# Sorting with the features stationary, a mixer tap on ScalarE, and direct turns at the end of a layer

## The chip, the cores and the metric

The program runs on one core of a Trainium2 chip, in one launch. A core has five engines that run their own instruction queues side by side and meet through semaphores: TensorE (PE, matrix products), VectorE (DVE), ScalarE (ACT), GpSimd (POOL) and SyncE (SP, which here only starts transfers). The metric is the device time of one execution in microseconds (us), compared as the median of several.

## The reference, cut to what matters

```python
x = x + quantised_product(layernorm(x), ctx)              # 1: int8-like fake quantisation, matmul
x = x + mixer(layernorm(x), ...)                          # 2: state-space mixer, 8 groups of 16 heads
x = x + experts(layernorm(x), ...)                        # 3: base matmul + top-2 of 8 LoRA experts
x = x + cloud(ctx, layernorm(x), ...)                     # 4: point cloud network, two layers
x = x + block_sparse_linear(layernorm(x), ...)            # 5
x = x + gated_ffn(layernorm(x), ...)                      # 6

# inside the mixer: a causal convolution with 4 taps, then silu
xBC = silu(conv(xBC, conv_w, groups=CONV_DIM) + conv_b)
L = exp(segment_sum(A * dt))                              # per head, 64 x 64, per batch
# inside the cloud: 4 sort orders of 1024 points from Morton and Hilbert keys of the coordinates
inds = [window(argsort(key)) for key in keys]             # windows of 10 neighbours in sorted order
g = [concat(center, feats[inds] - center) for inds ...]   # 1024 points x 10 rows x 512 channels
out = softmax(q @ q.T / 8) @ q ; fused = out @ W_lin.T + b
h = lrelu(instance_norm(conv1x1(fused))).max(over the 10)
```

The mixer sees T = 128 tokens (2 batches of 64) and the cloud 2 batches of 1024 points with 64 features each.

## The kernel before, in words

Every stage is a block of its own, one instruction stream for each engine, written by hand; nothing is scheduled by a tool. A block ends when all engines have reached its end (a barrier). Waits on semaphores (`pe.wait_ge(s_x, n)`) set the order between the engines. `hold_clock` (L100) issues idle products of the identity on PE, in fives (HOLD = 5), to keep PE's granted clock up.

**Stage 1** computes the quantised product; at its end PE runs 8 x HOLD idle passes of two each while DVE adds the result to x and takes the norm's statistics.

**Mixer.** PE projects the normalised x by the streamed weights (L530) for two B and two C chunks of 4 blocks and then for each of the 8 groups for two halves of x (bank 0 and 1) and two halves of the gate. ACT copies each projected chunk out of PSUM into a padded buffer (L643 `xpad`) and signals `s_evac`; DVE convolves the 4 taps of 4 blocks, 16 instructions a chunk: the newest tap with the bias by L751, the three others by L753. A chunk of PSUM may be written again once `s_evac` has come. `segments()` (L572) makes the cumulative sums of the decays as two products of 128x512, whose right side `seg_rhs` GpSimd builds from `adt_tok`. `out_projection` (L560) multiplies by `w_out`, streamed into `wt`. DVE also computes the 30-bit sort keys in between (class `SortKeys`, small chained instructions on 128x32 integers), three bits in the head, two inside group 0 and four bits and the final assembly between group 0 and group 1; `parg`, the parameters of a group, is copied at a group's start (L810). Ranks are counted by DVE within groups 1 to 7 (L781). Groups 1 to 6 are a loop.

**Experts.** 32 base products (L973), then the transposed `mid` and the adapters (L979).

**Cloud, layers 1 and 2.** The layer opens with the products of the layer's weights (L1388 to L1391), then sorts. A sort is a product with one-hot matrices: DVE builds 64 one-hots of 128 x 1024 (L1633: `iota == rank`), and PE multiplies for each of 8 phases (batch, method) 8 chunks of points by 8 chunks of ranks in two parts (high and low half of the float), with the one-hot as the stationary side and 64 feature columns moving (L1416: 128 products of 64 columns a phase). ACT evicts each phase (L1547). After four phases PE transposes the result (L1427) into `sortedT`, in which features lie on partitions and ranks run along the row. 32 transfers put the unsorted rows into `fTr`.

Then 43 steps of 24 points run as a software pipeline. For step it: POOL subtracts the centre (L1765 `X`), PE computes scores (L1453) and turned rows (L1466), DVE takes the maximum and subtracts it (L1679, L1681), ACT takes exp (L1582), DVE the sums (L1701) and reciprocals, POOL normalises (L1783), ACT and POOL split P into a high and a low half (L1575, L1790), DVE turns P (L1694 into `P_turned`) and SP moves it by 4 transfers to `PT`; 4 steps behind the scores PE multiplies P by the rows (`weighted_rows`, L1482, "PV" below), ACT unloads the result (L1561), 5 steps behind PE applies the linear map (`linear`, L1498 and L1505 or, in layer 2, L1501), 6 steps behind DVE takes statistics and the maximum over the 10 (`reduce`, L1661 and L1667). `PT` and the banks of the linear map exist twice. Ten small copies by DVE (`edges`, L1645 to L1649) fill the windows at both ends of the sorted rows; they follow the turn of step 0. The last steps, with no new scores, are the drain. A layer ends with the instance norm: all 43 statistics are merged (L1717), then 1024 columns are normalised and passed through the leaky relu (L1727, L1730).

## Time and profile before

| | us |
|---|---|
| median of 3 runs | 1089.07 |
| lowest and highest | 1088.49 and 1091.02 |
| the profiled execution | 1092.99 |
| its span | 1091.4 |
| busy: PE, DVE, ACT, POOL | 1017.7, 786.2, 427.0, 439.9 |

The stages are, from the barriers in the timelines: quantised product to 43.65, mixer to 487.2, experts to 511.3, layer 1 to 746.8 (its steps from 556), layer 2 to 1009.7 (its steps from 790.8), the cloud's output to 1019.9, the last two operators to 1091.4. In the profile PE is the matrix engine, PEld its weight loads, PEq its queue. In a timeline a row gives the start, the duration, the engine, the line, the operation with output and inputs, the number of like instructions in a row, and in brackets how long the engine had been idle and what ended that. PE's rows end a little after the next one's start, so the difference of starts is the better price of a run of products.

### The profile page before, as it was taken

The page shows a single profiled execution, that of the slowest core. Times are in us where ns is not written, and L with a number is a line of the kernel's source. Part 1 is how long each engine was busy: PE and PEld are TensorE (multiplying, and loading weights), DVE is VectorE, ACT ScalarE, POOL GpSimd, SP SyncE. Part 2 cuts the span into 40 slices and gives each one's busy share as a digit, 9 for nine tenths or more (in the row PEclk, how much of TensorE's full clock was granted, in tenths as well). Part 3 has the DMA queues.
Part 4 walks back from the last instruction along what each step waited for, and adds up shares of the span by engine and source line. Part 5 has one row for each costly group of instructions (what it writes and reads, how often), then busy time and mean ns, then how long its engine had stood idle before and what let it go on. Part 6 is the DMA issues. An engine that isn't in the chain of part 4 may idle for free. (4 is left out here: it accounts for less than half of the span.)

```text
span 1091.4 us, 38562 instructions
## 1 busy us (share of the span) xinstructions
PE 1017.7 (93%) x16213; PEld 777.1 (71%) x16213; DVE 786.2 (72%) x1981; ACT 427.0 (39%) x621; POOL 439.9 (40%) x410
## 2 busy tenths in 40 slices
PE   4899987999999999989989999998989999999998
PEld 1798864977869688746877777768876666665585
DVE  7499897848567493864857999975679888896310
ACT  6112212222223313211246777762247666773010
POOL 1101252120202202110058999970169888886000
PEclk9999988999999999999999999999999999999989
DMA  8995774778778695284502222233212222221550
GB/s 336 379 369 210 260 268 153 296 248 330 288 293 308 239 338 196 84 342 193 85 13 61 69 69 69 68 76 58 44 27 66 58 58 58 59 60 37 221 242 20
DMA packets 58362, 181.39 MB, mean 166 GB/s; under 512 B 10041, under 2 KB 10793, under 8 KB 57898
## 3 DMA queue, kind: packets, MB, share of 16 engines
q1 hardware_dynamic: 55850, 171.80, 45.8%
q0 software_dynamic: 2432, 8.42, 2.4%
q8 instruction: 63, 1.03, 0.4%
q14 instruction: 17, 0.14, 0.0%
HBM read 150.26 MB, written 0.56 MB: 138 GB/s over the span
## 5 line engine op out<-in xcount | busy, mean ns | idle before, releaser
L530 PEld LDWEIGHTS ps<-hT,ring 128*128 128x128 f32 x2304 | 258.8, 192 | 3.5 <-issue 3.3
L530 PE MATMUL ps<-hT,ring 128*128 128x128 f32 x2304 | 259.2, 275 | 0.0
L1765 POOL TENSOR_TENSOR X<-sortedT,ring 128x960 f16 (+1 forms) x84 | 156.1, 1858 | 0.0
L909 POOL TENSOR_TENSOR y_y<-y_z,sgate 128x512 f32<-128x512 f32 x16 | 20.0, 1268 | 221.4 <-DVE y_z L840 204.4
L560 PE MATMUL ps<-wt,y_n 128*128 128x512 f32 x224 | 102.6, 612 | 0.0
L1783 POOL TENSOR_TENSOR S<-S,den 128x480 f32<-128x480 f32 x86 | 85.8, 998 | 37.9 <-DVE den L1703 37.8
L1790 POOL TENSOR_TENSOR PP<-S,PP 128x480 f16<-128x480 f32 x86 | 97.0, 1128 | 3.5 <-ACT PP L1575 3.5
L1482 PE MATMUL ps<-PT,ring 128*64 128x120 f16 x2752 | 96.2, 222 | 1.9 <-DMA PT<-P_turned 1.9
L1482 PEld LDWEIGHTS ps<-PT,ring 128*64 128x64 f16 x2752 | 81.9, 110 | 14.4 <-DMA PT<-P_turned 6.1
L1575 ACT CAST PP<-S 128x480 f16<-128x480 f32 x86 | 66.8, 777 | 61.5 <-POOL S L1783 61.5
L1561 ACT COPY OT<-ps 128x960 f32<-128x960 f32 x86 | 81.1, 943 | 17.3 <-PE ps L1482 17.3
L1567 ACT COPY ring<-ps 128x1024 f16<-128x1024 f16 x86 | 87.1, 1013 | 0.0
L560 PEld LDWEIGHTS ps<-wt,y_n 128*128 128x128 f32 x224 | 43.0, 197 | 49.0 <-issue 48.9
L1501 PE MATMUL ps<-OT,WN 128*128 128x480 f32 x172 | 76.3, 566 | 0.0
L1679 DVE TENSOR_REDUCE mx<-ps 128x16 f32<-128x480 f32 x86 | 55.8, 648 | 22.8 <-PE ps L1453 19.4
L1661 DVE BATCH_NORM_STATS2 stats<-ps 128x240 f32 (+2 forms) x129 | 47.9, 400 | 30.3 <-PE ps L1501 20.4
L1582 ACT ACTIVATE S<-S 128x480 f32<-128x480 f32 x86 | 51.3, 597 | 44.8 <-DVE S L1681 44.8
L1694 DVE STREAM_TRANSPOSE P_turned<-PP 128x512 f32<-128x512 f32 x86 | 60.7, 706 | 9.9 <-PE ps L1482 7.6
L100 PE MATMUL ps<-ident 128*128 128x128 f32 x460 | 59.2, 288 | 4.9 <-PEq L1290 3.2
L100 PEld LDWEIGHTS ps<-ident 128*128 128x128 f32 x460 | 56.8, 203 | 9.4 <-issue 8.4
L1701 DVE TENSOR_REDUCE den<-S 128x16 f32<-128x480 f32 x86 | 56.1, 652 | 8.8 <-ACT S L1582 5.1
L1416 PE MATMUL ps<-ring 128*128 128x64 f16 x2048 | 61.0, 193 | 1.3 <-issue 1.0
(316 smaller groups left out, 1637.4 us busy)
## 6 DMA issues: line engine op xcount, KB each, us to landing
ring<-in_w_in SPq DMA_DIRECT2D x36, 2048.0 KB, 9.1
wt<-in_w_out SPq DMA_DIRECT2D x16, 2048.0 KB, 7.9
PT<-P_turned SPq DMA_DIRECT2D x344, 64.0 KB, 2.0
ring<-in_w SPq DMA_DIRECT2D x8, 1024.0 KB, 11.9
ctx_chunks<-in_ctx SPq DMA_DIRECT2D x4, 1024.0 KB, 9.0
ring<-in_ctx SPq DMA_DIRECT2D x4, 1024.0 KB, 16.7
krow<-keys_scratch POOLq DMA_DIRECT2D x8, 512.0 KB, 4.9
mchunk<-in_mask_t POOLq DMA_DIRECT2D x8, 512.0 KB, 8.3
```

What stands on the lines that cost most here:

```text
L100: nc.tensor.matmul(k.ps[:, bank, 0:P], k.ident[:, :], k.ident[:, :], start=True, stop=True)
L530: mm = nc.tensor.matmul(ps[:, bank, j * T:(j + 1) * T], weights[:, j, kc * P:(kc + 1) * P], k.hT[:, kc, :], start=kc == 0, stop=kc == KC - 1)
L560: mm = nc.tensor.matmul(ps[:, bank + c, :], rows[:, j, :], k.wt[:, j, c * HALF:(c + 1) * HALF], start=j == 0, stop=j == GB - 1)
L1416: mm = nc.tensor.matmul(ps[:, (i + halves[0]) % 2, pt * C:(pt + 1) * C], c.perm[:, perm_buffer(layer, j), pt * P:(pt + 1) * P], c.spl[:, s ...
L1482: mm = nc.tensor.matmul(ps[half, O_BANK + slot // 4, at:at + 4 * ROWS], XR[:, slot, half], PT[:, :, r * SLOTS + slot, 0:ROWS, part], start ...
L1501: mm = nc.tensor.matmul(H, c.WN[:, a, 0, :], OT[:, a, :, :], start=False, stop=a == 1)
L1561: sc.copy(c.OT[ph % 2][:, :, :, :].rearrange("p a b n -> p a (b n)"), ps[:, O_BANK:O_BANK + 2, 0:2 * COLS]).then_inc(s_O, 1)
L1567: sc.copy(c.XR[ph][:, :, :].rearrange("p s d -> p (s d)"), xt[ph % 2]).then_inc(s_XR, 1)
L1575: sc.copy(c.PP[ph % 2][:, :, 0:ROWS, 0], c.S[ph % 2][:, :, :]).then_inc(s_hi, 1)
L1765: ins = gp.tensor_tensor(fcopy(c.X[u][:, 0, 0:1], full(cnt)), fcopy(c.fsT[:, 0, bass.ds(it * STEP, 1)], trio(start, cnt, 1)), fcopy(c.fTr[ ...
L1783: gp.tensor_tensor(S, S, fcopy(c.den[ph % 2][:, :], [[1, 2 * SLOTS], [0, ROWS]]), ALU.mult).then_inc(s_P, 1)
L1790: gp.tensor_tensor(PP[:, :, 0:ROWS, 1], c.S[ph % 2][:, :, :], PP[:, :, 0:ROWS, 0], ALU.subtract).then_inc(s_lo, 1)
```

## The change

What it does, stage by stage.

- **Stage 1 and mixer's head.** The idle passes at the end of stage 1 go from 8 x HOLD to 2 x HOLD, and 4 x HOLD open the mixer on PE.
- **Convolution.** The newest tap and the bias are computed by ACT (`newest_tap`: four ACTIVATEs with scale and bias, straight from PSUM), which gives `s_evac` after it; DVE has 12 instructions a chunk. For a group's first half ACT waits for `parg`.
- **Keys.** 16 instead of 17 chained instructions a bit; one bit moves from the stretch between groups 0 and 1 to the middle of group 0's convolution (so three there and three behind it). `adt_tok` is copied ahead of `dt_tok`, in another order of heads.
- **segments().** One small product, then four products of 64x64 tiles and 512 columns in place of two of 128x128; for the second half of the heads the two batches stand swapped, from a third transposed matrix `dtp`.
- **Last group.** Its `w_out` goes into `ring[8:16]` ahead of time; its last product is issued by column halves, so that DVE updates and measures the first half of x while PE computes the second.
- **Experts.** The base products of the second half are spread around the two waits for `mid`; the first layer's weight products and the block sums move here from the head of layer 1, and layer 2's to the end of layer 1.
- **Sort.** The features are the stationary side (128x64, batch 0 on the array's left columns and PSUM partitions 0 to 63, batch 1 on the right) and the one-hots move, 512 columns at a time. A phase is one method for both batches. The last method of layer 1 is split by ranks into `head` (256) and `rest` (768); layer 2 runs the methods backwards and splits the first (rest, then head) and the last (head, then rest). ACT evicts four groups of 32 partitions a phase, and transfers of SP put them into `sortedT`, for the head half of them by ACT. No transposes are left in the sort. The centre rows go through DRAM with 4 + 8 transfers.
- **Steps.** The ten edge copies go to ACT, two or so a step, in steps 1 to 3. X, S, OT and P_turned are in shared memory.
- **Drain.** The last two turns (steps 41 and 42) write `PT` directly, by four transposes of 32 partitions and no transfer. From step number 43 on DVE turns before it reduces, and PE applies `linear` before `weighted_rows`.
- **End of a layer.** The first 38 statistics are merged during the drain; the leaky relu runs by halves.

```diff
-            hold_clock(nc, k, 0, 8 * HOLD)
-
-
-
-
-KEY_STEPS = 10 + 7 + (BITS - 1) * (3 * 3 + 2 * 4) + 2 + 8 + 8 + 2 + 2 + 1
+            hold_clock(nc, k, 0, 2 * HOLD)
...
+            hold_clock(nc, k, 0, 4 * HOLD)
...
+                parts = [(j, c) for j in range(4 * h, 4 * h + 4) for c in range(2)]
+                if bank == 0 and h:
+                    parts.sort(key=lambda x: x[1])
+                for j, c in parts:
+                    mm = nc.tensor.matmul(ps[:, bank + c, :], rows[:, j, :], weights[:, j, c * HALF:(c + 1) * HALF],
+                                          start=j == 0, stop=j == GB - 1)
+                    if bank == 0 and j == GB - 1 and c == 0:
+                        mm.then_inc(s_out, 1)
...
                 pe.wait_ge(s_rhs, g + 1)
+                nc.tensor.matmul(ps[:, 2, 0:1], tri_gt[:, :], ones[:, :], start=True, stop=True)
                 for h in range(2):
-                    mm = nc.tensor.matmul(ps[:, 2 + h, :], tri_gt[:, :], seg_rhs[:, 8 * h:8 * h + 8, :], start=True, stop=True)
+                    for b in range(B):
+                        at = b if h == 0 else 1 - b
+                        rows, cols = slice(at * L, (at + 1) * L), slice(b * L, (b + 1) * L)
+                        mm = nc.tensor.matmul(ps[cols, 2 + h, :], tri_gt[rows, cols], seg_rhs[rows, 8 * h:8 * h + 8, :], start=True, stop=True)
...
+            def newest_tap(bank, half, params):
+
+                for j in range(4):
+                    ins = nc.scalar.activation(xc[:, 4 * half + j, :], ps[:, bank, j * T:(j + 1) * T], ACT.Identity,
+                                               bias=params(j, CK), scale=params(j, CK - 1))
...
+                    if h == 0:
+                        act.wait_ge(s_pg, g + 1)
+                    act.wait_ge(s_silu, 2 * g + 3 + h)
+                    newest_tap((G0 + h) % 2, h, lambda i, c: parg[:, 4 * h + i, c:c + 1])
...
+                for i in range(CK - 1):
+                    tap = CK - 2 - i
...
-                            ins = vec.tensor_scalar(dst, src, params(j, tap), params(j, CK), ALU.mult, ALU.add)
-                        else:
-                            ins = vec.scalar_tensor_tensor(out=dst, in0=src, scalar=params(j, tap), in1=dst, op0=ALU.mult, op1=ALU.add)
-                        ins.then_inc(s_cv, 1)
+                        vec.scalar_tensor_tensor(out=dst, in0=src, scalar=params(j, tap), in1=dst, op0=ALU.mult, op1=ALU.add).then_inc(s_cv, 1)
...
+                    if first and h == 0:
+                        keys.transform([BITS - 4])
...
+            base(0, range(KC))
+            base(1, range(0, 3))
             pe.wait_ge(s_r, 12)
             nc.tensor.transpose(ps[:, 5, 0:P], mid[:, :], k.ident[:, :]).then_inc(s_mt, 1)
+            base(1, range(3, 5))
             pe.wait_ge(s_mc, 1)
-            for c in range(2):
-                nc.tensor.matmul(ps[:, 3 + c, :], midT[:, :], k.ring[:, 10, c * HALF:(c + 1) * HALF], start=False, stop=True).then_inc(s_out, 1)
-            hold_clock(nc, k, 7, 2 * HOLD)
+            adapters(0)
+            base(1, range(5, KC))
+            adapters(1)
+            weight_products(nc, pe, k, 1)
+            nc.tensor.matmul(ps[:, 7, 0:KC * 32], k.cloud.blocks[:, :], k.msum[:, :], start=True, stop=True).then_inc(k.block_sums, 1)
+            hold_clock(nc, k, 2, HOLD)
...
-                            mm = nc.tensor.matmul(ps[:, (i + halves[0]) % 2, pt * C:(pt + 1) * C], c.perm[:, perm_buffer(layer, j), pt * P:(pt + 1) * P],
-                                                  c.spl[:, s, t, b * C:(b + 1) * C], start=at + pt + s == 0,
-                                                  stop=at == NT - 1 and pt == NT - 1 and s == 1)
...
+                for lo, hi, bank in sorted_pieces(i, kind):
+                    for part in range(2):
+                        for x in range(B):
+                            b = sort_order(layer, j + x)[0]
+                            perm = (c.heads[:, (j + x) % PER_METHOD, lo:hi] if kind == "head" else c.perm[:, perm_buffer(layer, j + x), lo:hi])
+                            mm = nc.tensor.matmul(ps[b * C:(b + 1) * C, bank, 0:hi - lo], c.spl[:, part, t, b * C:(b + 1) * C], perm,
+                                                  start=first and part == 0, stop=last and part == 1)
+                mm.then_inc(s_ord, 1)
...
+                if isinstance(it, int) and it >= STEPS:
+                    linear(*lagged(LINEAR_LAG))
...
+                for b in range(B):
+                    for a in range(2):
+                        rows = slice((b * 2 + a) * 2 * CH, (b * 2 + a + 1) * 2 * CH)
+                        ins = sc.mul(c.gathered[:, i % 2, a * B + b, begin:end],
+                                     ps[rows, bank:bank + 2, :].rearrange("p a n -> p (a n)")[:, 0:end - begin], 1 / SCALE)
...
+                if isinstance(it, int) and 1 <= it <= 3:
+                    next(edge, None)
...
+                if direct(it):
+                    v.wait_ge(s_PV, t0 + it - 1)
+                    for q in range(4):
+                        quad = slice(32 * q, 32 * q + 32)
+                        vec.transpose(words(c.PT[ph % 2][quad, q]), words(c.PP[ph % 2][quad])).then_inc(s_PT[ph % 2], 16)
+                    return
...
+                last_turns = isinstance(it, int) and it >= STEPS
+                if last_turns:
+                    turn(*lagged(TURN_LAG))
                 reduce(*lagged(REDUCE_LAG))
+                if last_turns:
+                    early_statistics(it)
                 shift(*lagged(0))
-                turn(*lagged(TURN_LAG))
+                if not last_turns:
+                    turn(*lagged(TURN_LAG))
                 denominators(*lagged(0))
...
+            pieces = [(half, b) for half in ((1, 0) if layer == 1 else (0, 1)) for b in range(nb)]
+            for i, (half, b) in enumerate(pieces):
+                piece = raw[:, b, half * HALF:(half + 1) * HALF]
+                vec.tensor_scalar(piece, piece, c.shift[:, b:b + 1], c.rsb[:, b:b + 1], ALU.subtract, ALU.mult).then_inc(s_end, 1)
+                v.wait_ge(s_end, nb + 2 + 2 * i + 1)
+                vec.scalar_tensor_tensor(out=piece, in0=piece, scalar=0.2, in1=piece, op0=ALU.mult, op1=ALU.max).then_inc(s_end, 1)
```

**ACT, the loop of the mixer's groups.** First the kernel before: the four copies of a group's two x halves, then the first gate; `m_proj` is a projection's end, `m_conv_step` DVE's convolution.

```order
L643 COPY xpad<-ps 128x4x64 [waits m_conv_step]
L643 COPY xpad<-ps 128x4x64
L676 REGISTER_ALU
L677 REGISTER_ALU [waits m_proj]
L643 COPY xpad<-ps 128x4x64 [waits m_conv_step]
L643 COPY xpad<-ps 128x4x64
L682 REGISTER_ALU
L684 REGISTER_ALU [waits m_proj]
L685 ACT_TABLE_LOAD
L685 ACTIVATE sgate<-ps 128x512 [waits m_y]
```

The same place after. L666 is the newest tap, `m_parg` the copy of the group's parameters by DVE.

```order
L660 COPY xpad<-ps 128x4x64 [waits m_conv_step,m_proj]
L660 COPY xpad<-ps 128x4x64
L666 ACTIVATE xc<-ps,parg 128x128 [waits m_silu,m_parg]
L666 ACTIVATE xc<-ps,parg 128x128 x3
L660 COPY xpad<-ps 128x4x64 [waits m_conv_step,m_proj]
L660 COPY xpad<-ps 128x4x64
L666 ACTIVATE xc<-ps,parg 128x128 [waits m_silu]
L666 ACTIVATE xc<-ps,parg 128x128 x3
L715 ACT_TABLE_LOAD [waits m_y]
L715 ACTIVATE sgate<-ps 128x512 [waits m_proj]
L672 ACTIVATE xsil<-xc 128x512 [waits m_conv_step,m_z]
```

Behind each pair of copies stand four ACTIVATEs, and the first of them waits for `parg`; the signal that frees the bank comes behind them.

**PE, the drain of layer 1.** Before: the last step that still has its own scores ahead (PV, then linear, L1482 and L1498 with L1505), and the start of the pieces that follow.

```order
L1482 MATMUL ps<-PT0,ring 64x120 [waits c_O,c_X_rows,c_P_placed0]
L1482 MATMUL ps<-PT0,ring 64x120 x31
L1498 MATMUL ps<-f16,WC1 128x240 [waits c_O,c_reduced]
L1498 MATMUL ps<-f16,WC1 128x240 x2
L1505 MATMUL ps<-OT1,WN 64x240 x4
L1482 MATMUL ps<-PT1,ring 64x120 [waits c_O,c_X_rows,c_P_placed1]
L1482 MATMUL ps<-PT1,ring 64x120 x31
L1498 MATMUL ps<-f16,WC1 128x240 [waits c_O,c_reduced]
L1498 MATMUL ps<-f16,WC1 128x240 x2
L1505 MATMUL ps<-OT0,WN 64x240 x4
L1482 MATMUL ps<-PT0,ring 64x120 [waits c_O,c_X_rows,c_P_placed0]
```

After, from the last linear of the steps with scores on:

```order
L1612 MATMUL ps<-f16,WC1 128x240 [waits c_O,c_reduced]
L1612 MATMUL ps<-f16,WC1 128x240 x2
L1619 MATMUL ps<-gathered,WN 64x240 x4
L1596 MATMUL ps<-PT1,ring 64x120 [waits c_O,c_X_rows,c_P_placed1]
L1596 MATMUL ps<-PT1,ring 64x120 x31
L1612 MATMUL ps<-f16,WC1 128x240 [waits c_O,c_reduced]
L1612 MATMUL ps<-f16,WC1 128x240 x2
L1619 MATMUL ps<-gathered,WN 64x240 x4
L1596 MATMUL ps<-PT0,ring 64x120 [waits c_O,c_X_rows,c_P_placed0]
L1596 MATMUL ps<-PT0,ring 64x120 x31
L1612 MATMUL ps<-f16,WC1 128x240 [waits c_O,c_reduced]
```

PV stood ahead of linear, now linear stands ahead of PV, and linear waits for DVE's reduction of two steps earlier (`c_reduced`).

**DVE, the same drain.** Before:

```order
L1661 BN_STATS stats<-ps 128x6 [waits c_H]
L1667 TENSOR_REDUCE ring<-ps 128x24
L1694 STREAM_TRANSPOSE P_turned1<-PP1 128x512 [waits c_P_placed1,c_P_low]
L1661 BN_STATS stats<-ps 128x6 [waits c_H]
L1667 TENSOR_REDUCE ring<-ps 128x24
L1694 STREAM_TRANSPOSE P_turned0<-PP0 128x512 [waits c_P_placed0,c_P_low]
L1661 BN_STATS stats<-ps 128x6 [waits c_H]
L1667 TENSOR_REDUCE ring<-ps 128x24
L1661 BN_STATS stats<-ps 128x6 [waits c_H]
L1667 TENSOR_REDUCE ring<-ps 128x24
```

After:

```order
L1848 TENSOR_REDUCE den0<-gathered 128x16 [waits c_exp]
L1850 RECIPROCAL den0<-den0 128x16 [waits c_den]
L1835 STREAM_TRANSPOSE PT1<-PP1 32x512 [waits c_PV,c_P_low]
L1835 STREAM_TRANSPOSE PT1<-PP1 32x512 x3
L1802 BN_STATS ring<-ps 128x6 [waits c_H]
L1808 TENSOR_REDUCE ring<-ps 128x24
L1835 STREAM_TRANSPOSE PT0<-PP0 32x512 [waits c_PV,c_P_low]
L1835 STREAM_TRANSPOSE PT0<-PP0 32x512 x3
L1802 BN_STATS ring<-ps 128x6 [waits c_H]
L1808 TENSOR_REDUCE ring<-ps 128x24
```

Before, the statistics (L1661) and the maximum (L1667) of a step precede the turn; after, the four direct transposes of 32x512 precede them, and they wait for `c_PV`, the PV that last read this `PT`.

## Rows read from the trace of the kernel before

**Rows 1.** windows of the whole span (their columns in the first line)

```profile
core 0: us, PE busy (x) PEld busy (x) DVE busy (x) ACT busy (x) POOL busy (x), PEclk, DMA share, GB/s
...
118.00:183.12 65.12, 52.45 (x376) 40.79 (x368) 58.78 (x184) 12.22 (x22) 25.03 (x44) 0.88 0.66 244
...
230.90:277.70 46.80, 46.68 (x368) 37.59 (x368) 31.19 (x97) 12.12 (x22) 7.98 (x8) 1.00 0.79 291
...
556.00:745.90 189.90, 178.54 (x5131) 131.17 (x5131) 159.99 (x317) 132.28 (x177) 165.28 (x136) 0.99 0.25 61
```

**Rows 2.** timeline, end of the first stage: start, us, engine, line, operation, [idle <-releaser]

```profile
34.30 9.10 PE L100 MATMUL ps<-ident 128*128 128x128 f32 x80
...
43.69 0.21 DVE L87 BATCH_NORM_AGGREGATE mv<-bn 128x2 f32<-128x12 f32 x1 [6.13 <-PEq L135]
```

**Rows 3.** timeline of PE, mixer, end of group 0's head

```profile
94.96 2.48 PE L572 MATMUL ps<-seg_rhs,tri_gt 128*128 128x512 f32 x4 [2.53 <-POOL seg_rhs L892]
```

**Rows 4.** timeline of PE, mixer, a steady group

```profile
229.58 1.16 PE L612 MATMUL ps<-MT,xs 64*64 64x64 f32 x64
230.88 1.98 PE L572 MATMUL ps<-seg_rhs,tri_gt 128*128 128x512 f32 x4
```

**Rows 5.** timelines of PE, DVE and ACT, mixer group 1

```profile
119.84 28.75 PE L530 MATMUL ps<-hT,ring 128*128 128x128 f32 x256
...
152.04 1.12 PE L594 MATMUL ps<-ident,xsil 128*128 128x128 f32 x4 [3.46 <-ACT xsil L649]
...
180.94 0.34 PE L608 MATMUL ps<-ones_col,xs 128*64 128x1 f32 x2 [7.00 <-DVE xs L832]
...
146.69 1.11 DVE L751 TENSOR_SCALAR xc<-xpad,parg 128x128 f32<-128x128 f32 x4 [0.23 <-DVE parg L810]
...
151.24 7.82 DVE L751 TENSOR_SCALAR xc<-xpad,parg 128x128 f32<-128x128 f32 x4
...
185.84 2.52 ACT L697 ACTIVATE y_n<-y_y,parg 128x128 f32<-128x128 f32 x8 [19.65 <-POOL y_y L909]
```

**Rows 6.** timeline of PE, mixer, its last two products

```profile
468.33 8.78 PE L560 MATMUL ps<-wt,xc 128*128 128x512 f32 x16 [2.46 <-DMA wt<-in_w_out]
...
477.10 7.11 PE L560 MATMUL ps<-wt,xc 128*128 128x512 f32 x16
```

**Rows 7.** timelines of PE, DVE and ACT, sort of layer 1

```profile
517.62 3.75 PE L1416 MATMUL ps<-ring 128*128 128x64 f16 x123
...
531.23 3.26 DVE L1633 TENSOR_SCALAR ring<-iota,rank 128x1024 f16<-128x1024 f16 x8
...
556.53 1.28 ACT L1582 ACT_TABLE_LOAD   x1
558.42 0.60 ACT L1582 ACTIVATE S<-S 128x480 f32<-128x480 f32 x1 [0.61 <-DVE S L1681]
```

**Rows 8.** timeline of PE at three places; last, groups of instructions (ACT)

```profile
23.57 1.03 PE L293 MATMUL ps<-q,onesz 128*128 128x512 bf16 x4
24.43 1.03 PE L293 MATMUL ps<-q,q1z 128*128 128x512 bf16 x4
...
730.10 1.03 PE L1505 MATMUL ps<-OT,WN 128*64 128x240 f32 x8
...
987.58 1.77 PE L1501 MATMUL ps<-OT,WN 128*128 128x480 f32 x4
...
L1561 ACT COPY OT<-ps 128x960 f32<-128x960 f32 x86 | 81.1, 943 | 17.3 <-PE ps L1482 17.3
```

**Rows 9.** timeline of POOL, first steps of layer 1

```profile
575.14 0.99 POOL L1783 TENSOR_TENSOR S<-S,den 128x480 f32<-128x480 f32 x1 [3.45 <-DVE den L1703]
```

**Rows 10.** timelines of PE and DVE, end of layer 1

```profile
728.61 1.14 PE L1482 MATMUL ps<-PT,ring 128*64 128x120 f16 x32 [0.22 <-DMA PT<-P_turned]
...
731.82 0.70 DVE L1694 STREAM_TRANSPOSE P_turned<-PP 128x512 f32<-128x512 f32 x1
...
741.88 1.32 DVE L1717 BATCH_NORM_AGGREGATE mvb<-stats 128x2 f32<-128x258 f32 x1
```

400 lines of the change are left out of this document (238 added, 162 removed).

## The prediction

> **What bounds the kernel now.** I read the windows of the span first, to see which engine is full in which stage, and then in each stage the timeline of the engine that is full, looking for rows with idle time in brackets. In a steady mixer group PE is busy 46.68 of 46.80 us [rows 1]: there only fewer or shorter products count. Group 1 is different: 65.12 us, PE busy 52.45 at a granted clock of 0.88 and DVE busy 58.78 [rows 1]; DVE bounds it. In layer 1's steps PE, DVE and POOL are all near full [rows 1], so a stall of any of them in the first steps is never made good. At stage ends everything is serial and the chain itself is the price.
>
> **Part by part** (negative is faster; the sum is made against the profiled execution, 1092.99 us, and carried over to the median, which is 3.9 lower).
>
> *Stage 1 to mixer, −3.0.* 80 idle passes take 9.10 us, 0.114 each, and DVE, done earlier, waits 6.13 for PE [rows 2]. DVE's idle time begins at 37.6; PE would end 60 passes sooner, at 36.6, so the barrier falls near 37.9. But 40 passes (4.55) now stand ahead of the norm's transposes: these start near 42.4 rather than 45.4. Between 0 (something else holds the barrier) and −6.
>
> *Head, −3.7.* PE waits 2.53 for `seg_rhs` [rows 3], which hangs on DVE's chain. DVE sheds four newest taps a chunk at 1.11 us [rows 5] and one link of each of the keys' bits; ACT takes four ACTIVATEs at 2.52/8 = 0.31 each [rows 5], 1.25 a chunk, with room. The wait goes (2.5), a smaller one before it too (0.5), and the first segments gain 0.7 (next).
>
> *segments(), −0.7 a group, −3.6 in five.* Four passes of 128x512 hold PE 1.8 us until the next row starts, 1.98 as the row has it [rows 4]. Now four 64x64 tiles of 512 columns. The same tiling shows 64 products of 64 columns in 1.16 us [rows 4]: 18 ns for 64 columns, against 0.45 x 64/512 = 56 ns at the untiled rate; so tiles do run at a time. Taken: 1.1 with the small product. If they overlap in twos only, the gain is 0.
>
> *Group 1, −7.1, the least certain of the mixer.* Before, DVE ends the keys, copies `parg` near 146.4, convolves (the start of its L751) [rows 5], is held up by POOL (a quartet of 7.82 instead of 1.11), counts ranks, and PE waits 3.46 for `xsil` and 7.00 for `xs` [rows 5], with further waits and half-clock stretches: 18.3 above a steady group. After, three effects. DVE's keys between the groups are some 20 links shorter (one bit of 17 moved, one link less in each of three), about 0.225 each, −4.5; −3.5 more goes with the quartets of L751 that DVE no longer has. Against it, ACT's first newest tap waits for `parg`, hence for the end of the keys, and behind it stands `s_evac`, hence PE's third projection: a projection takes 28.75/4 = 7.2 us [rows 5], and two of them end 14.4 after the first began; before, `parg` came 28.4 after the group's start (146.4 − 118.0), now some 5.5 sooner (those links, and group 0's convolution ends sooner by the taps it has shed), at 22.9, and the tap takes 1.25: PE stalls some 9.9 us in mid-group, where before it ran on to its later waits. These later waits go, being the same lateness. I make the group 58.0. Ends: 66 (both stalls stay) and 52.
>
> *Last group, −5.1.* The wait for `w_out` (2.46) goes and 8.78 becomes 7.11 [rows 6], −3.9 with the small gap before; the split update hides half of the last update, −0.5; segments −0.7.
>
> *Experts, −1.4.* Two waits around `mid` are filled; 2.0 us of weight products move here from layer 1. The barrier is about 0.3 later, and layer 1's transposes 1.8 earlier.
>
> *Sort, −5.6 and −1.2.* Before, 123 products of 64 columns take 3.75 us, 30.5 ns each, and the sort runs from 517.62 to the first exp at 558.42, 40.8 us [rows 7]. Its products are 1024 x 30.5 = 31; the rest is eviction, transposes and POOL. After, 256 products of 512 columns, in pairs on the two column halves. A 16-bit pass of 512 columns costs 0.215 (four in 0.86, the difference of two starts [rows 8]). Do halves overlap? Eight half-array passes of 240 take 1.03, four whole ones of 480, as many columns, 1.77 [rows 8]. Yes, nearly: 128 pairs x 0.215 = 28 us. DVE builds a one-hot in 3.26/8 = 0.41 [rows 7], two an item, 0.82 beside PE's 0.86; with the weights' 2.2 us in between DVE is about even. The tail: head evicted and moved during the rest; rest evicted in four pieces of 768 columns, at 943 ns for 960 [rows 8] about 3.1; then the table load, 1.28 [rows 7], which now stands behind the wait for the shift and so on the path (before it hid there: exp still waited 0.61 after it). Start to first exp 35.2. Layer 2 has 86 builds (about 31 us with its weights 34), DVE bounds it: 37.7 for 38.9.
>
> By the Trainium skill ("TensorE: Matmul & The Clock Gate", Part 3, Packing small matmuls) a weight load overlaps products in flight only if its row group differs; column halves share all rows, so a pair would not overlap. The rows just cited [rows 8] show that such pairs do, so the sum does not use it; it is the first rival below. The skill also ("ScalarE: Activation LUTs", What ACT_TABLE_LOAD costs) gives 2.66 us for a table switch with its drain; by it the load on the path would cost 1.4 more in each layer, and our trace cannot show that, as DVE was waited for there.
>
> *Early steps, −5.0 and −4.4.* Edge copies on DVE delay the reciprocals, and POOL waits 3.45 for one [rows 9] and about a unit less two steps on; there are two such waits a layer, 6.0 us together. ACT, the least busy engine here, takes the copies in three steps; X(0) to X(6) do not need the last of them. POOL bounds layer 1's steps, so what it no longer waits is won; I leave 1 for the start of PV, and a little more in layer 2, where PE is nearer to the bound.
>
> *Drain, +7.6 and +9.5.* Here the change is costly. A turn of 128x512 takes 0.70 [rows 10]. Its length is that of a row, 512, so I price one of 32x512 at 0.65 and four at 2.6, against 0.70 and a transfer of about 2 that DVE need not sit through. Moreover the new order chains: PV(39) → turn(41), which waits for it → reduce(37) (0.75) → linear(39), which waits for that and now precedes PV(40) → PV(40) → turn(42) → reduce(38) → linear(40) → PV(41) → unload → linear(41) → PV(42) → unload → linear(42) → reduce. Linear is 1.4 (1.03 of it [rows 8]), PV 1.1 [rows 10], unload 1.0 [rows 8]. 2.6+0.75+1.4+1.1+2.6+0.75+1.5+1.0+1.05+1.4+1.1+1.0+1.5+0.7 = 18.45, from PV(39)'s end near 731.05: 749.5, where before the last reduction ended at 741.88, where the merge starts [rows 10]. In layer 2 linear is 2.1 (1.77 and the smaller part before it) [rows 8], reduce 1.25, and two merges stand on DVE: +9.5. Ends: a turn of 32 partitions for a quarter (0.2), then +1.2 and +3; and transposes of 0.8, +9 and +11.
>
> *Ends of layers, −1.8 and −0.55.* The merge of 1.32 [rows 10] shrinks to 0.3; the relu in halves costs 0.4 more; the weight products (2.6) lie ahead of the barrier.
>
> Sum: −3.0 −3.7 −3.6 −7.1 −5.1 −1.4 −5.6 −1.2 −5.0 −4.4 +7.6 +9.5 −1.8 −0.55 = **−25.4**: the profiled execution 1067.6, the median **1063.7 us**.
>
> **Rivals.** *Pairs in the sort do not overlap* (the skill's rule). 28 us a layer become 55; the sort would end 27 later in each, less little, 1063.7 + 54 = about 1118: slower than before. It decides from the point where a pair takes over 1.45 single passes. Against it: the half-array rows. For it: those have short moving sides. *The drain is cheap.* Turns at 0.2 or PE's order harmless: +17 becomes 0 to 4: about 1048. For it: the old drain has a transfer on the path at each of the last turns. *Group 1's stall adds up* with the later waits: +8, about 1072. *DVE or ACT bounds the sort*, the builds not streaming beside evictions: +4 a layer, also about 1072.
>
> **How the numbers follow.** The forecast (1054 to 1070) 0.55; the cheap drain 0.18; the last two together 0.17; serial pairs 0.06; something unseen that makes it slow 0.04. For 8 in 10 the range needs the forecast, most of the cheap drain and the two at 1072: **1047 to 1076**. A measurement here can tell 0.2%, 2 us, from nothing. Faster by more: 0.89; the same: 0.02; slower: 0.09.
>
> **What would show it.** Sort: L1538 at 0.86 per item of four pairs, and the first exp 35 after the first product. Early steps: no POOL row with a wait of over 1 us. Group 1: PE idle about 10 us ahead of its third projection (L535), released by ACT. Drain: L1835 at 0.6 to 0.7 and PE waiting for `c_reduced`, 18 us from PV(39) to the last reduction. Wrong it would be if the two drains together cost less than 8, or a pair of products more than 0.3.

## The result, and the profile after

The changed kernel takes **1097.31 us** (median of four runs, 1096.82 to 1099.03) against 1089.86 for the kernel before beside it: a ratio of 1.0072, interval 1.0054 to 1.0090. It is slower by 0.7%, where 1063.7 us was forecast. The profiled execution is one of 1099.03 us with a span of 1097.4 and a mean granted clock of 0.964 (before: 1092.99, 1091.4 and 0.980).

The program is serial between its stages, so both traces can be cut at the same events. "First exp" is ACT's first of 128x480; "PV(39)" is the last pass of L1596 (before: L1482) but three, the one that the drain starts from; "last reduction" is the last of DVE's statistics of a layer.

| Stretch (us) | before | after | measured | predicted |
|---|---|---|---|---|
| start to the first product of sort 1 | 517.62 | 494.95 | -22.7 | -23.9 |
| sort 1: first product to first exp | 40.80 | 49.01 | **+8.2** | -5.6 |
| first exp to the end of PV(39) | 171.33 | 168.13 | -3.2 | -5.0 |
| drain: to the last reduction | 12.09 | 24.05 | **+12.0** | +7.6 |
| last reduction to sort 2 | 12.40 | 8.80 | -3.6 | -1.8 |
| sort 2: first product to first exp | 38.89 | 44.39 | **+5.5** | -1.2 |
| first exp to the end of PV(39) | 194.10 | 193.01 | -1.1 | -4.4 |
| drain: to the last reduction | 15.15 | 29.03 | **+13.9** | +9.5 |
| last reduction to the end | 89.02 | 86.03 | -3.0 | -0.55 |

(The predicted -23.9 is -3.0 -3.7 -3.6 -7.1 -5.1 -1.4.) The profiled execution missed its forecast of 1067.6 by 31.4 us: 20.5 in the two sorts, 8.7 in the two drains, 5.1 in the steps and 1.2 ahead of the sort; the ends of layers give 4.2 back.

Each stretch comes from one execution, so its noise has to be known. Seven kernels have the same new sort with the same transfers (the changed one, e4, e7, e8, e9, e10 and e13), and yet their first sort lasts 46.36 to 49.12 us and their second 40.97 to 44.39. The old second sort took 38.89 in every one of its four traces.

**The mixer** did what was forecast. The timeline of PE (start, us, engine, line, operation, [idle before <-releaser]) shows the new products of `segments` at 1.09 (1.2 with the small product ahead of them, from 89.67 to 90.89, where 1.1 was taken; they answer to L572 in [rows 4]), no wait ahead of it (2.53 in [rows 3]), and in group 1 the stall that the first newest tap makes, 9.79 for a forecast of 9.9:

```profile
89.88 1.09 PE L589 MATMUL ps<-seg_rhs,tri_gt 64*64 64x512 f32 x8
...
136.22 17.35 PE L535 MATMUL ps<-hT,ring 128*128 128x128 f32 x128 [9.79 <-ACT xc L666]
```

Group 1 and a steady group, as windows (us, busy time and instructions of PE, PEld, DVE, ACT and POOL, granted clock, DMA share, GB/s), 59.4 us for a forecast of 58.0, and 46.4 for 46.1 ([rows 1] has 65.12 and 46.80). So a steady group gains 0.4 and not the 0.7 that `segments` was to give:

```profile
110.54:169.91 59.37, 49.37 (x380) 40.23 (x375) 47.19 (x157) 14.91 (x30) 23.75 (x44) 0.89 0.65 233
170.00:216.40 46.40, 46.26 (x375) 37.30 (x375) 27.74 (x89) 14.93 (x30) 7.99 (x8) 1.00 0.78 293
```

**The sort** is where the forecast broke. The timelines of PE, SP, ACT and POOL in layer 1 (they answer to [rows 7]):

```profile
494.95 20.91 PE L1538 MATMUL ps<-ring 128*64 128x512 f16 x192
...
494.95 23.07 PE L1538 MATMUL ps<-ring 128*64 128x512 f16 x224
518.27 3.36 PE L1538 MATMUL ps<-ring 128*64 128x512 f16 x37 [0.25 <-DVE ring L1785]
...
540.14 0.39 PE L1557 MATMUL ps<-mask_cols,mask_rows 64*128 64x240 bf16 x2 [15.14 <-POOL X L1926]
...
495.84 3.51 SPq L1469 DMA_DIRECT2D cloud_rows<-h_sb  x4
501.48 3.60 SPq L1474 DMA_DIRECT2D ring<-cloud_rows  x8
...
526.67 5.66 ACT L1675 ACTIVATE gathered<-ps 32x1024 f32<-32x1024 f32 x8 [13.58 <-DMA sortedT<-gathered]
...
542.67 1.28 ACT L1728 ACT_TABLE_LOAD   x1 [6.24 <-DVE gathered L1822]
543.96 0.60 ACT L1728 ACTIVATE gathered<-gathered 128x480 f32<-128x480 f32 x1
...
538.12 3.70 POOL L1926 TENSOR_TENSOR X<-sortedT,ring 128x960 f16<-128x960 f32 x2 [71.70 <-DMA sortedT<-gathered]
```

The first row is a shorter window on the same products. It holds the 192 of 512 columns, and the row of 224 has 32 of 256 columns behind them. The products themselves are as forecast: the first of 256 columns starts at 515.69, so 96 pairs took 20.74 us, 0.216 a pair against the 0.215 of one full pass, and the two column halves run side by side. The last products are done near 525. Then PE stands still for 15.14 us. ACT could not evict before 526.67, because it waits 13.58 us for a transfer that is to free `gathered`, and the first X starts at 538.12, behind transfers again. The windows of the same places show the reason:

```profile
501.50:527.00 25.50, 22.21 (x230) 12.47 (x226) 21.09 (x69) 8.45 (x9) 0.00 (x0) 1.00 1.01 120
527.00:538.00 11.00, 0.00 (x0) 0.00 (x0) 0.00 (x0) 8.44 (x12) 0.00 (x0) 0.54 0.53 72
```

By their share all DMA engines are busy (1.01), and they move only 120 GB/s; a steady mixer group gets 293 at a share of 0.78. And the transfers of 256 KB take 11 us each (DMA issues by size: queue, count, KB each, median us to landing):

```profile
ring<-cloud_rows SPq DMA_DIRECT2D x16, 256.0 KB, 10.8
...
sortedT<-gathered SPq DMA_DIRECT2D x12, 256.0 KB, 11.4
```

**The drain** is the chain that the prediction wrote down, and longer. PE in layer 1:

```profile
711.00 1.09 PE L1596 MATMUL ps<-PT,ring 128*64 128x120 f16 x32
715.96 0.78 PE L1612 MATMUL ps<-f,WC 128*128 128x240 f16 x3 [3.86 <-DVE ring L1808]
716.67 1.87 PE L1619 MATMUL ps<-gathered,WN 128*64 128x240 f32 x8
718.32 1.38 PE L1596 MATMUL ps<-PT,ring 128*64 128x120 f16 x32
723.55 0.78 PE L1612 MATMUL ps<-f,WC 128*128 128x240 f16 x3 [3.85 <-DVE ring L1808]
```

and DVE, whose turn of 128x512 takes 0.70 in [rows 10]:

```profile
712.24 2.90 DVE L1835 STREAM_TRANSPOSE PT<-PP 32x512 f32<-32x512 f32 x4 [2.51 <-PE ps L1596]
...
719.84 2.90 DVE L1835 STREAM_TRANSPOSE PT<-PP 32x512 f32<-32x512 f32 x4 [3.94 <-PE ps L1596]
```

PE waits for `reduce`, DVE waits for `PV`, in turn. A turn of a quarter of the partitions takes 2.90/4 = 0.725, as long as a whole one. And behind PE's waits its granted clock falls, to 0.66, 0.74 and 0.50 in windows of 5 us (0.50 is 1.2 GHz throughout), where a `linear` (0.78 + 1.87) and a PV are nearly twice as long:

```profile
710.00:715.00 5.00, 2.09 (x43) 1.52 (x40) 2.67 (x4) 2.26 (x3) 1.92 (x2) 1.00 0.19 44
715.00:720.00 5.00, 3.74 (x43) 2.43 (x43) 1.03 (x4) 0.26 (x1) 0.00 (x0) 0.66 0.01 3
720.00:725.00 5.00, 1.45 (x7) 0.81 (x9) 4.84 (x9) 0.69 (x1) 0.00 (x0) 0.74 0.00 0
725.00:730.00 5.00, 3.86 (x43) 2.59 (x41) 1.14 (x6) 0.96 (x1) 0.00 (x0) 0.50 0.00 0
```

### The profile page after: what moved, and what is told of

The parts are those of the page before. It is cut to its first block and busy times, and to the rows that moved or that the text cites. A ratio compares the mean times of both kernels' runs of the same rounds, so it can differ in the third digit from the quotient of the medians.

```text
span 1097.4 us, 35638 instructions
## 1 busy us (share of the span) xinstructions
PE 999.8 (91%) x14728; PEld 740.2 (67%) x14728; DVE 756.4 (69%) x1950; ACT 475.1 (43%) x733; POOL 437.5 (40%) x404
## 5 line engine op out<-in xcount | busy, mean ns | idle before, releaser
L1926 POOL TENSOR_TENSOR X<-sortedT,ring 128x960 f16 (+2 forms) x86 | 160.3, 1865 | 142.4 <-DMA sortedT<-gathered 142.4
L1707 ACT COPY gathered<-ps 128x960 f32<-128x960 f32 x86 | 81.2, 944 | 45.0 <-PE ps L1596 45.0
L1596 PE MATMUL ps<-PT,ring 128*64 128x120 f16 x2752 | 100.1, 226 | 0.0
L1944 POOL TENSOR_TENSOR gathered<-gathered,den 128x480 f32<-128x480 f32 x86 | 86.4, 1004 | 33.4 <-DVE den L1850 33.4
L1951 POOL TENSOR_TENSOR PP<-gathered,PP 128x480 f16<-128x480 f32 x86 | 97.6, 1135 | 3.5 <-ACT PP L1721 3.5
L782 DVE SCALAR_TENSOR_TENSOR xc<-xpad,parg,xc 128x128 f32<-128x128 f32 x192 | 58.2, 366 | 56.5 <-ACT xc L666 55.3
L1596 PEld LDWEIGHTS ps<-PT,ring 128*64 128x64 f16 x2752 | 86.1, 113 | 13.6 <-issue 5.3
L1721 ACT CAST PP<-gathered 128x480 f16<-128x480 f32 x86 | 67.1, 780 | 58.2 <-POOL gathered L1944 54.4
L1615 PE MATMUL ps<-gathered,WN 128*128 128x480 f32 x172 | 79.5, 587 | 0.0
L1848 DVE TENSOR_REDUCE den<-gathered 128x16 f32<-128x480 f32 x86 | 56.0, 651 | 10.7 <-ACT gathered L1728 7.7
L1841 DVE STREAM_TRANSPOSE gathered<-PP 128x512 f32<-128x512 f32 x82 | 57.8, 705 | 7.7 <-PE ps L1596 2.8
L1538 PE MATMUL ps<-ring 128*64 128x512 f16 (+1 forms) x608 | 57.2, 347 | 3.6 <-DVE ring L1785 2.6
```

What stands on the lines that cost most here:

```text
L782: vec.scalar_tensor_tensor(out=dst, in0=src, scalar=params(j, tap), in1=dst, op0=ALU.mult, op1=ALU.add).then_inc(s_cv, 1)
L1596: mm = nc.tensor.matmul(ps[half, O_BANK + slot // 4, at:at + 4 * ROWS], XR[:, slot, half], PT[:, :, r * SLOTS + slot, 0:ROWS, part], start ...
L1615: mm = nc.tensor.matmul(H, c.WN[:, a, 0, :], OT[:, a, :, :], start=False, stop=a == 1)
L1707: sc.copy(c.OT[ph % 2][:, :, :, :].rearrange("p a b n -> p a (b n)"), ps[:, O_BANK:O_BANK + 2, 0:2 * COLS]).then_inc(s_O, 1)
L1721: sc.copy(c.PP[ph % 2][:, :, 0:ROWS, 0], c.S[ph % 2][:, :, :]).then_inc(s_hi, 1)
L1841: vec.transpose(words(c.PC[ph % 2]), words(c.PP[ph % 2])).then_inc(s_turned, 1)
```

## Theories

*Sort.* Theory: the transfers bound it, and of these the eight that read the centre rows from DRAM (8 x 256 KB a layer, to 16 partitions at a time) stand ahead of the sorted rows (as many bytes again). Rivals: DVE's builds bound it; or the cost is one queue's and a second queue cures it. *Drain.* Theory: the new order on PE and DVE chains them; direct turns are innocent. Rivals: the direct turns are dear by themselves; or one engine's order alone does it. *Mixer.* Theory: it is worth its 22 us alone; rival for what is left in group 1: DVE's chain of keys and not the place of the `parg` copy.

## The experiments

Each ratio is to the kernel before, run beside it, with its 95% interval. In the texts on record "L1" and "L2" are the layers. Line numbers in rows are those of the kernel named.

### e1: no centre rows

It leaves out both legs of the centre rows and the wait for them, so POOL subtracts what happens to lie in `fTr`.

```diff
-                    sp.dma_start(c.rows_kept[to:to + 2 * CH, :], src[at:at + 2 * CH, :]).then_inc(c.kept, 16)
-            sp.wait_ge(c.kept, 64 * layer)
-            for r in range(2):
-                for m in range(NM):
...
-                                         ap=[[N, CH], [2 * CH * N, 2 * B], [1, N]])).then_inc(s_cc, 16)
...
-            pool.wait_ge(s_cc, cc0 + 16 * 2 * NM)
```

> The changed kernel without the centre rows' transfers of both layers (4 into DRAM, 8 back a layer) and without the wait for them, so the centres subtracted are stale: the output is not the reference's. Queue theory: these 8 transfers of 256 KB stand ahead of the sorted rows' transfers on the same queue and take some 17 us a layer at the 120 GB/s of that stretch; without them the sorted rows land as they are made, and first product to first exp falls from 49.0 to about 36 us in layer 1 and from 44.4 to about 37 in layer 2; the whole about 20 less than the changed kernel's 1097.3, 1077. Rival, that each sorted transfer is slow for itself (landing 11 us in the median): those stretches fall by under 4 us each, and the time stays above 1090.

Measured: 1086.55 us, 0.9996 [0.9972, 1.0020], 0.8% less than the changed kernel's 1.0072, some 8 us where 20 were expected. Sort 1 fell from 49.01 to 38.34; sort 2 took 42.72, which is no change, for it lies among the 40.97 to 44.39 of the kernels that have the centre rows. In layer 1 the theory holds: 10.7 of the 13.8 us missed there come from the centre rows (8.0 to 10.8 against the seven kernels). In layer 2 it was wrong by 5.7: there the last products end 32.3 after the first without the centre rows as well, since DVE builds 86 one-hots ahead of them, and the sorted rows still have to land (X starts 4.6 later, at 771.21). PE's wait behind the last product is 6.62 here, 9.81 in the changed kernel and 6.43 in e13, which has the centre rows. What is left in layer 1, 38.3 for a forecast of 35.2, is a landing too: the head's two transfers wait behind the 512 KB of the method before it. The timelines of PE and POOL (layer 1, layer 2):

```profile
529.17 0.38 PE L1546 MATMUL ps<-mask_cols,mask_rows 64*128 64x240 bf16 x2 [5.74 <-POOL X L1914]
...
771.21 3.71 POOL L1914 TENSOR_TENSOR X<-sortedT,ring 128x960 f16<-128x960 f32 x2 [69.34 <-DMA sortedT<-gathered]
```

### e2: centre rows to 64 partitions at a time

```diff
-                for m in range(NM):
-                    to = r * C + m * CH
-                    sp.dma_start(c.fTr[to:to + CH, :, :],
...
-                                         ap=[[N, CH], [2 * CH * N, 2 * B], [1, N]])).then_inc(s_cc, 16)
+                for x in range(2 * B):
+                    sp.dma_start(c.fTr[r * C:(r + 1) * C, x, :],
+                                 bass.AP(tensor=c.rows_kept.tensor, offset=c.rows_kept.offset + (r + 2 * x) * CH * N,
+                                         ap=[[0, NM], [N, CH], [1, N]])).then_inc(s_cc, 16)
```

> The changed kernel with the centre rows' 8 transfers a layer cut the other way: each still has 64 rows of 4 KB, 256 KB, but they go to 64 partitions and not to 16. Theory that a transfer to 16 partitions is held to about 120 GB/s by the few partitions it writes: the 8 take some 9 us rather than 17, the sort shortens by about 8 in layer 1 and 5 in layer 2, the whole to about 1084. Rival, that bytes or packets alone count: no change, 1097.

Measured: 1110.41 us, 1.0235 [1.0207, 1.0263]; sorts of 56.67 and 50.23. The edit did not do what it was meant to. In the window of its transfers most DMA engines stand idle:

```profile
500.00:505.00 5.00, 5.00 (x50) 2.61 (x48) 4.83 (x17) 4.06 (x4) 0.00 (x0) 1.00 0.19 50
```

A share of 0.19 at 50 GB/s. So this says nothing on partitions; e5 takes the two apart. (The Trainium skill, "DMA: Bandwidth & Descriptors", Why a DMA increments its semaphore by 16 and not by 1, has the number of engines follow from the outermost dimension of the access pattern; here that is 4, a quarter of 16, and the trace agrees with 0.19 here and 0.23 in e5.)

### e3: half of the sorted rows by ACT's queue

```diff
-                    for r in range(2):
-                        place_sorted(sp, i, r, SPANS["full"]).then_inc(c.landed[i], 16)
+                    place_sorted(sp, i, 0, SPANS["full"]).then_inc(c.landed[i], 16)
...
+                if i < NM - 1:
+                    place_sorted(act, i, 1, SPANS["full"]).then_inc(c.landed[i], 16)
```

> The changed kernel with half of the sorted rows' transfers (those to partitions 64 and up) started by ScalarE instead of SyncE, so that the two halves of a phase, on other partitions, can run at a time. By the partition theory a phase's 512 KB take 2.2 to 3 us rather than 4.4, but still stand behind the centre rows in the 16 engines: 4 to 8 us less over both layers, about 1091. By the theory that only bytes count: nothing gained, and ScalarE's issues cost about 0.7 each, 1098 to 1100.

Measured: 1095.66 us, 1.0090 [1.0054, 1.0126], sorts of 48.40 and 42.92, both within what the untouched sort takes. The rate goes from 120 to 135 GB/s and no gain can be told from nothing: a second queue is no cure. That the limit lies behind the queues is what e5 measures.

```profile
501.50:525.00 23.50, 21.36 (x222) 12.04 (x218) 20.29 (x67) 7.91 (x8) 0.00 (x0) 1.00 0.99 135
```

### e4: the old order in the drain, direct turns kept

```diff
-                if isinstance(it, int) and it >= STEPS:
-                    linear(*lagged(LINEAR_LAG))
-                    weighted_rows(*lagged(PV_LAG))
-                else:
-                    weighted_rows(*lagged(PV_LAG))
-                    linear(*lagged(LINEAR_LAG))
+                weighted_rows(*lagged(PV_LAG))
+                linear(*lagged(LINEAR_LAG))
...
-                last_turns = isinstance(it, int) and it >= STEPS
+                last_turns = False
...
-                if last_turns:
+                if isinstance(it, int) and it >= STEPS:
```

The last pair of lines keeps the early statistics, which hung on the same name; e7 to e11 have it too wherever `last_turns` is False.

> The changed kernel with the drain's old order in both layers (reduce before turn on VectorE, PV before linear on PE), the direct turns kept. Theory that the order makes one serial chain of the drain: from the end of PV(39) to the last reduction falls from 24.0 to about 12 us in layer 1 and from 29 to about 16 in layer 2, PE's clock does not fall to its lower level, and the whole is about 24 less, 1073. Rival, that four turns of 32 partitions (2.90 us) are what costs: the gain is under 6, above 1091.

Measured: 1068.24 us, 0.9828 [0.9807, 0.9850]: 2.4% or about 27 us faster than the changed kernel (1.0072) by the order of two calls on each engine. Drains of 12.40 and 16.04 (from 24.05 and 29.03), 24.6 together; the steps to PV(39) 0.6 and 2.2 shorter, as `linear(38)` no longer stands ahead of it. PE's rows of the drain now follow each other, and the clock stays high (a `linear` of 0.48 + 1.03, for 0.78 + 1.87):

```profile
711.07 0.48 PE L1612 MATMUL ps<-f,WC 128*128 128x240 f16 x3
711.48 1.03 PE L1619 MATMUL ps<-gathered,WN 128*64 128x240 f32 x8
712.34 1.14 PE L1596 MATMUL ps<-PT,ring 128*64 128x120 f16 x32
```

### e5: the transfers by themselves

Everything but transfers is left out. Eight forms of moving 2 MB follow each other, each ending before the next begins:

```diff
+            for r in range(2):
+                for m in range(4):
+                    sp.dma_start(dst[r * C + m * CH:r * C + m * CH + CH, 0:4, :], dram(r * CH * N, [[N, CH], [2 * CH * N, 4], [1, N]])).then_inc(s_a, 16)
+            settle(8)
...
+            for m in range(4):
+                sp.dma_start(dst[:, m:m + 1, :], k.wt[:, m:m + 1, :]).then_inc(s_a, 16)
+            settle(4)
```

> Nothing but transfers: all of the network's work is left out and x is copied to the output. Eight sorts of transfers one after the other on SyncE's queue, each sort to its end before the next: (1) DRAM to 16 partitions x 4 rows of 4 KB, 8 of 256 KB, as the changed kernel's centre rows; (2) DRAM to 64 partitions x 1 row; (3) the same with the 64 partitions as 4 times the same 16 rows; (4) SBUF 16 partitions to 16, 4 rows each, as the sorted rows; (5) SBUF 64 to 64; (6) SBUF 128 to 128, 512 KB; (7) as 4 but from and to the same partitions; (8) as 4 in 32 pieces of 64 KB, as the kernel before. Theory that few destination or source partitions hold a transfer to about 120 GB/s: 1, 4 and 7 take 16 to 18 us each for their 2 MB (about 120 GB/s), 2 and 5 about 9 (240), 6 about 6. Rival, that SBUF-sided small rows or the queue are at fault: 1, 2, 4, 5 and 6 are all alike. Sort 3 is slow by too few engines in both (about 100 GB/s).

Measured in one execution, in windows (here: us, busy POOL, clock, DMA share, GB/s), in this order: (1) DRAM to 16 partitions, as the centre rows; (2) DRAM to 64 partitions; (3) the same as 4 x 16, as in e2; (4) 16 partitions to 16 others, as the sorted rows; (5) 64 to 64; (6) 128 to 128; (7) 16 to the same 16; (8) form 4 in 32 pieces of 64 KB:

```profile
14.24:33.67 19.43, 0.00 (x0) 1.00 0.89 108
33.67:45.73 12.06, 0.00 (x0) 1.00 0.79 174
45.73:69.94 24.21, 0.00 (x0) 1.00 0.23 87
69.94:89.03 19.09, 0.00 (x0) 1.00 0.83 110
89.03:100.04 11.01, 0.00 (x0) 1.00 0.81 191
100.04:106.82 6.78, 0.00 (x0) 1.00 0.78 309
106.82:125.59 18.77, 0.00 (x0) 1.00 0.84 112
125.59:147.96 22.37, 0.00 (x0) 1.00 0.63 94
```

The rate follows the number of partitions: about 110 GB/s for 16 whether the source is DRAM or SBUF, 174 to 191 for 64, 309 for 128. The 4.19 MB of a layer at 110 to 120 are 35 to 38 us, as long as the whole sort was meant to take (35.2). (The Trainium skill, "SBUF — State Buffer", Door 1: The DMA port swizzle, gives 16 partitions four of 16 ports, 104 GB/s measured at 1 MiB, and 64 partitions eight, 196. The rows agree: 108 to 112, and 174 to 191. Read before the forecast, this section would have priced the transfers.)

### e6: the mixer's part alone

The kernel before with all the edits of stage 1 and the mixer, and none of the experts or of what follows. The first of them:

```diff
-            hold_clock(nc, k, 0, 8 * HOLD)
+            hold_clock(nc, k, 0, 2 * HOLD)
...
+            hold_clock(nc, k, 0, 4 * HOLD)
```

> The kernel before with stage 1's and the mixer's part of the change alone (experts, sort, steps, drain and layer ends as before). If the stages are worth what the two traces say when read up to the sort, it is 21 us faster than the kernel before, ratio 0.981; the prediction's own terms give 22.5. Rival, that early starts in the mixer are given back later (weights that land no earlier): under 15.

Measured: 1067.42 us, 0.9800 [0.9777, 0.9824], 21.8 us faster than before; the first product of the sort comes at 495.80, 0.9 later than with the experts' edit too. From the first base product of the experts (470.63 here, 471.14 in the changed kernel) it is 25.17 against 23.81, so their edit is worth 1.4. What follows the mixer then costs the changed kernel 2.7%, some 30 us.

### e7: the old order and no direct turns

```diff
-LAST, DIRECT = 3, 2
+LAST, DIRECT = 3, 0
...
-                last_turns = isinstance(it, int) and it >= STEPS
+                last_turns = False
```

> The changed kernel with the drain's old order and without direct turns (all turns go through the transfers again), early statistics kept. If the order was the whole loss, it stands within 3 us of the run with the old order and direct turns, which had 0.9828 of the kernel before; if direct turns save the transfers they are meant to save, it is 2 to 4 slower than that; if four turns of 0.73 on VectorE cost more than a turn and a transfer, 1 to 3 faster.

Measured: 1067.07 us, 0.9796 [0.9768, 0.9825]; drains of 15.01 and 16.42 for e4's 12.40 and 16.04, 3.0 more, and the same time within the intervals. Its first sort took 46.36 for 48.97, which makes up for the drains; the edit does not touch the sort, and why its length varies stays open. Nor are the 3.0 the worth of direct turns alone: in this run the early statistics (1.18) stand ahead of the last turn, PE waits 2.24 for the transfer behind it, and the PV that follows takes 1.55. In e12, with transfers as well but the turn ahead of the statistics, that wait is 1.13, the PV takes 1.10 and the drain 12.34.

### e8: the parameters of group 1 earlier

Old order in the drain; `parg` is copied after the first of the remaining bits of the keys, so that ACT's newest tap need not wait for their end. (The later groups' copies move to the end of the group before.)

```diff
-            keys.transform(range(BITS - 7, 0, -1))
+            keys.transform([BITS - 7])
+            group_parameters(1)
+            keys.transform(range(BITS - 8, 0, -1))
```

> The changed kernel with the drain's old order, and with the copy of group 1's parameters moved up: VectorE makes it after the first of the three remaining key bits, not after all of them and the final assembly. Theory that PE's 9.8 us in group 1 are ScalarE's tap waiting for that copy: PE's idle time at its third projection goes, the group shortens from 59.4 to 50 or 52 us, and the ratio to the kernel before falls from 0.9828 to 0.975. Rival, that VectorE's chain bounds the group anyway: the wait reappears at xsil or xs, gain under 3 us.

Measured: 1069.79 us, 0.9829 [0.9808, 0.9850], e4's time. The stall of 9.79 is gone from PE's third projection and stands ahead of the products with `xs` instead; DVE had itself waited for the keys to come back from DRAM (timelines of PE and of DVE):

```profile
167.45 0.34 PE L625 MATMUL ps<-ones_col,xs 128*64 128x1 f32 x2 [10.22 <-DVE xs L866]
...
151.11 1.28 DVE L808 TENSOR_SCALAR_CACHE_REDUCE junk<-krow,kcol 128x1024 bf16<-128x1024 f32 x1 [7.98 <-DMA krow<-keys_scratch]
```

The rival's outcome came: the group is bound by DVE's chain, and moving the copy only changes which of its waits PE sees. The link that binds is another one, though. Here DVE waits 7.98 for `krow`, up to 151.11, while in the changed kernel the same instruction starts at 146.56 with no wait. What the group would take if the keys came back sooner was not run.

### e9 and e10: each engine's order alone

e9 has the old order on DVE and the new one on PE:

```diff
-                last_turns = isinstance(it, int) and it >= STEPS
+                last_turns = False
```

> The changed kernel with the drain's old order on VectorE alone (reduce before turn); PE keeps linear before PV. Theory that the two new orders make the long chain only together, since linear(39) waits for reduce(37), which waits behind turn(41), which waits for PV(39): with this link gone, from PV(39)'s end to the last reduction takes about 16 us in layer 1 (24.0 with both new, 12.4 with both old) and 21 in layer 2; the ratio to the kernel before is near 0.992. Rival, that PE's order alone makes the chain: no change from 1.0072.

Measured: 1075.87 us, 0.9878 [0.9827, 0.9929]; drains of 14.19 and 20.06. e10 has it the other way round:

```diff
-                if isinstance(it, int) and it >= STEPS:
-                    linear(*lagged(LINEAR_LAG))
-                    weighted_rows(*lagged(PV_LAG))
-                else:
-                    weighted_rows(*lagged(PV_LAG))
-                    linear(*lagged(LINEAR_LAG))
+                weighted_rows(*lagged(PV_LAG))
+                linear(*lagged(LINEAR_LAG))
```

> The changed kernel with the drain's old order on PE alone (PV before linear); VectorE keeps turn before reduce. By the same theory PV(40) no longer stands behind linear(39), so turn(42) follows turn(41) and one reduction at once: 14 us in layer 1 and 18 in layer 2, ratio near 0.987. Rival, that VectorE's order alone makes the chain: no change from 1.0072.

Measured: 1070.36 us, 0.9839 [0.9788, 0.9890]; drains of 13.36 and 17.33. Above e4's drains, PE's order alone costs 1.8 and 4.0, DVE's alone 1.0 and 1.3, together 8.1; both at once cost 24.6. It is the two orders together that make the chain: either engine in the old order has work to do while the other's result is on its way.

### e11: centre rows spread through DRAM

e4 and e3, and the centre rows written four times to DRAM, so that they can be read back by plain transfers of 64 partitions.

```diff
+            for m in range(NM):
+                sp.dma_start(bass.AP(tensor=c.rows_kept.tensor, offset=c.rows_kept.offset + m * CH * N,
+                                     ap=[[C * N, 8], [N, CH], [1, N]]), src[:, :]).then_inc(c.kept, 16)
...
+                        at = (b * 4 + a * 2 + r) * C
+                        sp.dma_start(c.fTr[r * C:(r + 1) * C, a * B + b, :], c.rows_kept[at:at + C, :]).then_inc(s_cc, 16)
```

> The changed kernel with the drain's old order, half of the sorted rows' transfers on ScalarE's queue, and the centre rows laid out four times in DRAM (4 transfers of 512 KB), so that the 8 transfers back are plain ones to 64 partitions. By the transfer measurement (2 MB in 12.1 us to 64 partitions, in 19.4 to 16) the centre rows are in some 4 us sooner although more is written first; first product to first exp falls from 49.0 to about 43 us in layer 1 and from 42.7 to 41 in layer 2: ratio 0.976 against 0.983 with the order alone. Rival, that the writes into DRAM eat the gain: 0.983.

Measured: 1078.29 us, 0.9909 [0.9883, 0.9936], slower than e4; sorts of 50.94 and 49.25, both longer than in any kernel with the untouched sort. The reads did get faster:

```profile
512.00:525.00 13.00, 10.99 (x128) 6.02 (x124) 10.35 (x37) 0.62 (x1) 0.00 (x0) 1.00 0.96 197
```

197 GB/s, as e5 has it; but they start only at 511.64, 16.3 us after the first write was issued at 495.35 (501.48 and 5.6 in the changed kernel). The four writes ate the gain, as the rival had it, and more.

### e12: the change without its sort and its drain

The kernel before with the mixer, the experts, the moved weight products, the edges on ACT, the early statistics and the leaky relu by halves; the sort, the turns and the orders of the drain stay the old ones.

```diff
+            def edges():
+
+                row = c.W
+                ends = lambda at, dims: fcopy(c.fsT[:, 0, at:], [[row, 4]] + dims)
+                act.wait_ge(s_sc, sc0 + 8)
...
+                if isinstance(it, int) and 1 <= it <= 3:
+                    next(edge, None)
```

> The kernel before with every part of the change but the new sort, the direct turns and the drain's new order: stage 1, mixer, experts, weight products ahead of the barriers, edge copies on ScalarE, early statistics, relu by halves. Sum from the runs: mixer 21, experts 1.4, early steps 3.8 and 3.3, layer ends 2 to 3 and 1 more than the mixer alone: 1089.5 less 33 is 1056, ratio 0.970. Rival, that the edge copies gained only because the new sort's late start gave them room: 1062, ratio 0.975.

Measured: **1055.14 us, 0.9696 [0.9657, 0.9735]**, with e14 the fastest of all: 3.0% below before and, by the two ratios, 41 us below the changed kernel. By stretch: 494.78 to the sort, sorts of 40.74 and 38.89, steps of 166.94 and 189.80 (-4.4 and -4.3, for the -5.0 and -4.4 forecast), drains of 12.34 and 15.04, and 8.71 from the last reduction to sort 2.

### e13: the clock held up through the drain

The changed kernel with ten idle products behind each of the later PVs.

```diff
                     linear(*lagged(LINEAR_LAG))
                     weighted_rows(*lagged(PV_LAG))
+                    if STEPS < it < STEPS + 4:
+                        hold_clock(nc, k, 1, 2 * HOLD)
```

> The changed kernel with both new orders in the drain, and 10 idle products (2.3 us) on PE behind the PVs of the three pieces from the second on, in the gaps where PE waits for VectorE; nothing else. Theory that 9 of the 26 us that the two drains lost are PE's products at 1.2 GHz after the first 4 us gap, on the serial chain: the later linears take 1.4 and not 2.4 us in layer 1, PV(39) to the last reduction falls from 24.0 to about 20 us there and from 29.0 to 25 in layer 2, the whole by 6 to 8, ratio near 1.001. Rival, that the chain alone is the loss and the clock costs nothing on it: no change, 1.007, or the idle products' own length on top.

Measured: 1095.35 us, 1.0065 [1.0042, 1.0087]; drains of 23.33 and 29.59. Not conclusive as a time, because the idle products stand on the chain themselves. The rows are of use: behind the idle products the same `linear` is back at its short time.

```profile
720.21 3.35 PE L100 MATMUL ps<-ident 128*128 128x128 f32 x20
724.13 0.48 PE L1612 MATMUL ps<-f,WC 128*128 128x240 f16 x3 [0.58 <-DVE ring L1810]
724.55 1.03 PE L1619 MATMUL ps<-gathered,WN 128*64 128x240 f32 x8
```

### e14: e12 with direct turns

```diff
+                if direct(it):
+                    v.wait_ge(s_PV, t0 + it - 1)
+                    for q in range(4):
+                        quad = slice(32 * q, 32 * q + 32)
+                        vec.transpose(words(c.PT[ph % 2][quad, q]), words(c.PP[ph % 2][quad])).then_inc(s_PT[ph % 2], 16)
+                    return
```

> The version with the old sort and drain and all the rest of the change (0.9696 of the kernel before), with the two last turns made directly, in the old order. By the spans of the runs with old order, with and without direct turns, the drain of layer 1 is 2.6 us shorter with them and that of layer 2 0.4: 1052, ratio 0.967. Rival, that those 2.6 us were only the later end of PV(39) in that run: no change, 0.970.

Measured: 1056.63 us, 0.9706 [0.9683, 0.9730], no change from e12, as the rival had it; drains of 12.07 and 16.03 (e12: 12.34 and 15.04). In the old order the direct turns win 0.3 in one layer and lose 1.0 in the other: four turns of 0.725 and no transfer are worth one turn of 0.70 and a transfer.

## Why the prediction was wrong, step by step

**Right: everything ahead of the sort**, -22.7 for -23.9, by its own steps: no wait for `seg_rhs`, a stall of 9.79 for 9.9, group 1 in 59.4 for 58.0; e6 shows the whole as a time. `segments` alone was priced too well, 0.4 a steady group for 0.7. The experts' part is 1.4 as forecast (e6's 25.17 against 23.81); stage 1 was not run apart.

**Wrong: the sort, by 20.5 us.** The step that failed is the tail: "head evicted and moved during the rest; rest evicted in four pieces". It has no term for the landing of the transfers, and the centre rows, which the change rereads through DRAM in 4 + 8 transfers, have no term in the sum at all. The working of PE, DVE and ACT in that step was sound (a pair at 0.216 for 0.215, builds bounding layer 2, the table load of 1.28 on the path; exp starts right behind it at 543.96, so the further 1.4 that the prediction set beside it did not come on the path). In its place the runs show: 2 MB of centre rows and 2 MB of sorted rows a layer, all into 16 partitions at a time, at 110 to 120 GB/s (e5, and the window at a share of 1.01). The centre rows cost 10.7 of the 13.8 us missed in layer 1, and nothing that can be told from nothing in layer 2 (e1). The rest, 3.1 there and the 6.7 of layer 2 (3.3 to 6.7 over the seven kernels), is the sorted rows' own landing behind the last phases: read from the rows, where POOL's first X waits for `sortedT`, not run apart, as no kernel had the new sort with wider transfers of its rows. Why that landing differs by over 3 us between kernels with the same sort is open. As it is built here the new sort loses, as e12 shows, whose old sort takes 40.74 and 38.89. Even without its centre rows (e1) it wins 2.4 in layer 1 and loses 3.8 in layer 2. Whether it would win with wider transfers is not shown.

**Mis-sized: the drain, by 8.7 us**, with the mechanism right (e4: 24.6 us come and go with the two orders; e9, e10: it takes both). The linear was priced at 1.4 and PV at 1.1 from rows at full clock. On the chain a linear lasts 2.35 three times (715.96 to 718.32, and twice more) for e4's 1.27, and the PVs behind them 1.38, 1.81 and 1.68. The chain was written down as 18.45 from PV(39)'s end, and it took 24.05, 5.6 more: going through it start by start, linears and PVs are 4.6 over their terms, the eight direct turns with their waits 0.8 (2.93 to 3.09 for 2.6 each time), all else 0.2. The table has 4.4 and not 5.6 for layer 1 because the prediction set PV(39)'s end at 731.05, 1.3 later than in the kernel before (728.61 + 1.14 in [rows 10]), and so put the `linear(38)` that now precedes it into the drain, where the table counts it among the steps. In layer 2 a linear was priced at 2.1 and lasts 4.1, two times over:

```profile
986.76 0.98 PE L1612 MATMUL ps<-f_both,WC 128*128 128x480 f16 x2 [4.42 <-DVE ring L1808]
987.54 3.41 PE L1615 MATMUL ps<-gathered,WN 128*128 128x480 f32 x4
990.88 1.59 PE L1596 MATMUL ps<-PT,ring 128*64 128x120 f16 x32
```

It follows from the chain itself: PE waits 3.86 to 4.42, the clock goes down, and the products behind are slow. That it is the clock shows in e1, e2 and e3, which have the same drain and need 22.78, 22.05 and 22.81 in layer 1 for 24.05. In all three `linear(41)`, behind the same wait of 1.14 to 1.15, is short again (0.47 + 1.03). Window and rows of the changed kernel, then of e1:

```profile
728.00:733.00 5.00, 4.02 (x43) 2.75 (x43) 0.72 (x2) 0.79 (x2) 0.00 (x0) 0.54 0.00 0
728.88 0.76 PE L1612 MATMUL ps<-f,WC 128*128 128x240 f16 x3 [1.14 <-ACT gathered L1707]
...
718.00:723.00 5.00, 3.47 (x54) 2.45 (x54) 0.72 (x2) 2.46 (x3) 0.00 (x0) 1.00 0.00 0
718.38 0.47 PE L1601 MATMUL ps<-f,WC 128*128 128x240 f16 x3 [1.15 <-ACT gathered L1696]
```

When the clock comes back within a drain differs from trace to trace; why was not studied. Of the two signs named that would refute the forecast, drains under 8 together or a pair over 0.3, neither came: it failed at a place that it had not named. The rival "the drain is cheap" falls, as do turns at 0.2.

**Steps, by 5.1.** "POOL bounds layer 1's steps, so what it no longer waits is won" holds: e12 gains 4.4 and 4.3 of 5.0 and 4.4. Of the two waits a layer for the reciprocals one is left, 1.63 at 562.73 and 1.59 at 808.07 (no row over 1 us was forecast). The changed kernel shows 3.2 and 1.1 because the drain's order already begins there: `linear(38)` ahead of PV(39) (e4 gets 0.6 and 2.2 of it back).

**Ends of layers**: -3.6 and -3.0 for -1.8 and -0.55. Of the first, about 2 us are not the change's: e6, whose code there is that of before, takes 10.34 for 12.40, since the products of that stretch ran at a granted clock of 1.00 and not 0.77 (before, then e6):

```profile
746.80:754.30 7.50, 7.50 (x54) 7.49 (x55) 1.29 (x2) 2.11 (x4) 0.00 (x0) 0.77 0.55 90
722.80:728.60 5.80, 5.80 (x52) 5.79 (x53) 1.29 (x2) 2.11 (x4) 0.00 (x0) 1.00 0.54 89
```

Against e6 the first gain is 1.5 (8.80), close to the 1.8 forecast, and e12 has it as well (8.71 to sort 2), so it doesn't hang on the drain. The second was worth more than forecast; its two merges shrink from 2.50 (e6) to 0.47.

**Rivals.** Serial pairs, the one way to a slower kernel that was written out (1118), did not come: the pairs overlap. "Something unseen that makes it slow", at 0.04, was what happened, and it was not unseen but unpriced: the diff has the transfers, and their sizes follow from it.

## What to carry to other kernels

When data is brought into another layout by transfers instead of by an engine, price them by bytes over the rate of the partitions that they touch (here 110 GB/s for 16, 309 for 128), all transfers of the stage together, and not by the landing time of a small one. When two engines alternate at the end of a loop, write the order of each beside the other and count the round trips: an order that is harmless on either engine can chain the two, and then the chain runs at the low clock as well. And of a change with many parts, run the parts: this one lost 0.7% as a whole, while without two of them it wins 3.0%. Before a stretch of one trace is explained, see how far it moves between kernels that share its code: here by up to 3.4 us.

## What the hardware showed that was not expected

- Transfers into 16 partitions run at 108 to 112 GB/s at a DMA share of 0.83 to 0.89 (e5): the share says nearly full while 309 GB/s are to be had with 128 partitions, at a share of 0.78. A share near 1 doesn't mean that much is moved.
- A source pattern whose outermost dimension is 4 uses a quarter of the engines (share 0.19 in e2 and 0.23 in e5, there at 87 GB/s).
- A turn of 32x512 takes 0.725, one of 128x512 0.70 [rows 10]: a quarter of the partitions saves nothing.
- Two products on the column halves of the array overlap: 0.216 a pair for 0.215 of one full pass. The rule of the Trainium skill that the prediction cites speaks of weight loads; that such pairs would not overlap was the prediction's inference from it, and the rows here decide against that.
- After PE had stood still for 3.86 us (712.1 to 715.96), the granted clock read 0.66 in the next 5 us and 0.50 in the window from 725, and a linear there took 2.35 us for 1.27.
